# Exponentials of the experts' softmax taken as powers of e on GpSimd instead of Exp on ScalarE

## The chip, the cores and the metric

One Trainium2 chip, one of its cores. The time is the device time of one launch in microseconds (us), the median of several runs. Beside the runs there is one profiled execution, with a record of every instruction and transfer.

## What is computed

`x` has 4096 rows of 128 features, `adj` is a 4096 x 4096 matrix of zeros and ones. Two blocks follow one another, each a graph attention and a feed-forward part, each added to `x`:

```python
x = x + _L0_gnn_ref(_layernorm(x, axis=-1), adj, L0_gnn_Wq, L0_gnn_Wk)
x = x + _L0_ffn_ref(_layernorm(x, axis=-1)[None], ...)[0]      # 30 steps of tanh, silu, layernorm, matmul
x = x + _L1_gnn_ref(_layernorm(x, axis=-1), adj, L1_gnn_Wq, ...)
x = x + _L1_ffn_ref(_layernorm(x, axis=-1)[None], L1_ffn_W1, ...)[0]
```

The change is in the last part, a layer of 8 experts of which each row uses the likeliest:

```python
H = jax.nn.gelu(xf @ W1 + b1, approximate=False)               # 512 hidden features
probs = jax.nn.softmax((H @ Wg + bg) / TEMP, axis=-1)          # 8 experts
assign = jnp.argmax(probs, axis=-1)
out = jnp.zeros_like(xf)
for e in range(Wd.shape[0]):
    y = H @ Wd[e] + bd[e]
    sel = (assign == e)[:, None]
    out = out + jnp.where(sel, probs[:, e:e + 1] * y, 0.0)
```

## The kernel before, in words

Every engine has a program of its own, written out by hand, and runs it in order; semaphores join them. The 4096 rows are 8 chunks of 512 rows (4 tiles of 128). The program has a preparation, the attention of block one (tiles named `a_`), the 30 steps (`r_`), the attention of block two (`b_`), and then the experts (class `Experts`; tiles `x_`, and many tiles of the attention under new names: `b_p_s` holds the hidden layer, `b_prob` gelu's result, `b_p_r` logits, ranks and the products, `b_gathered` the logits of a chunk, experts along the partitions). The experts go through the rows twice.

**The first pass** decides for each row which expert it goes to. Chunk by chunk TensorE turns the normalised rows (`turn_rows`, L1524), multiplies them by W1 in three float16 products for each of 4 parts (`layer`, L1535 to L1537), multiplies gelu's result by Wg in float32 (`logits`, L1547), turns the logits (`turn_logits`, L1558) and counts ranks (`ranks`). ScalarE rounds the turned rows to float16 (`front`, L1636), takes four gelus (`gelu`, L1645), and, two chunks late, the exponentials of the shifted logits, 4 tiles x 8 experts = 32 columns (`exps(c)`, L1661). Gelu and exp are in different tables of ScalarE, so an ACT_TABLE_LOAD stands before each change. VectorE, in `vector`, does per turn `c` of its loop: `copy_logits(c-1)`, `rows_low(c+2)`, `places(c-2)`, `weigh(c-2)`, `choose(c-1)`, `rows(c+3)`. `choose` (L1728 to L1744) takes the maximum, writes `shifted` (L1735) and the chosen expert; `places` gives each row its place in the sorted order; `weigh` (L1765 to L1770) waits for the exponentials, sums them over the 8 experts, inverts the sum and writes it, as the gate, into the packed row.

GpSimd copies x into the packed rows (`copy_x`, L1900), inverts the deviations of the last chunk once VectorE has measured them (`invert_rows`, L153 to L158, the last of the three a power of 4 columns), and sends each chunk's rows to their places in memory: `send(c)` waits for `weighed` of the chunk, then issues four indirect DMAs (L1907). Its loop before:

```python
        invert_rows(k, self.x_stats, pool, CHUNKS - 1)
        for c in range(CHUNKS):
            if c + 2 < CHUNKS:
                copy_x(c + 2)
            send(c)
```

The chunks are in two sets, 0 to 2 and 3 to 7. When a set is sent and its table of tiles is made (`table`, on VectorE), the queue of SP loads the sorted rows of that set, group by group (`sync`, L1495 and L1496).

**The second pass** takes 13 groups of up to 4 tiles of sorted rows: turned, multiplied by W1 and through gelu again, split in a high and a low part (`highs` on ScalarE, L1654; `lows` on VectorE, L1821), multiplied by the weights of the one expert of each tile (`products` on TensorE, L1586 to L1592), weighted by the gate and added to x (`send_back`, L1831), and scattered to the output by GpSimd (`store`, L1914). At the seam of the passes ScalarE takes `exps(5)` before the first two gelus of group 0, `exps(6)` after them and `exps(7)` after the group's last high part; VectorE does `weigh(7)` and `table(1)` between the low parts of group 0 and those of group 1. One more exponential, the elu of the attention's last chunk (`elu(CHUNKS - 1)`, L804), is taken by ScalarE in the turn c == 1 of the first pass.

Of the kernel before, what the change touches and what calls it, by code (L numbers as in the profile page):

```python
# [19 lines left out]

# [1 line left out]

# [7 lines left out]
ALU = mybir.AluOpType  # L32
ACT = mybir.ActivationFunctionType
# [3 lines left out]
P = 128  # L37
# [4 lines left out]
CHUNKS = N // CHUNK  # L42
TPC = CHUNK // P
# [5 lines left out]
E = 8  # L49
# [98 lines left out]
def invert_rows(k, s, pool, g):  # L148

    nc = k.nc  # L150
    var, padded = s["variance"][:, 0], s["variance"][:, 1]
    pool.wait_ge(s["measured"], TPC // 2 * (g + 1))
    nc.gpsimd.tensor_tensor(var.rearrange("p (a b) -> p a b", b=2), k.x_stats[:, ds(TPC // 2 * g, TPC // 2), 2:6:3],  # L153
                            k.inv_d[:].rearrange("p (a b) -> p a b", b=2), ALU.mult).then_inc(s["inverting"], 1)
    pool.wait_ge(s["inverting"], 3 * g + 1)
    nc.gpsimd.tensor_tensor(padded, var, k.eps[:], ALU.add).then_inc(s["inverting"], 1)
    pool.wait_ge(s["inverting"], 3 * g + 2)
    nc.gpsimd.tensor_tensor(k.rstd[:, ds(TPC * g, TPC)], padded, k.minus_half[:], ALU.pow).then_inc(s["inverting"], 1)  # L158
    pool.wait_ge(s["inverting"], 3 * g + 3)
# [164 lines left out]
def normalise_a(k, adj, adj_in):  # L324
# [6 lines left out]
    nc, io = k.nc, k.io  # L331
    with ExitStack() as ctx:
# [10 lines left out]
        s = {n: k.sem("a_" + n, ctx) for n in names}  # L343
# [26 lines left out]
        def _(dve):  # L370
# [4 lines left out]
            nc.vector.memset(k.ones_bf[:], 1.0)  # L375
            nc.vector.memset(k.ones[:], 1.0)
            nc.vector.memset(k.shift[:], SHIFT)

            nc.vector.memset(k.row_hi[:, :, D - 1:D], 1.0)
            nc.vector.memset(k.row_lo[:, :, D - 1:D], 0.0)  # L380
# [1047 lines left out]
class Experts:  # L1428
# [199 lines left out]
    def scalar(self, act, elu):  # L1628
        k, s, nc = self.k, self.s, self.k.nc

        def front(n):
            act.wait_ge(s["ft_ready"], n + 1)
            if n > 1:
                act.wait_ge(s["h_ready"], HC * (n - 1))
            wide = slice(0, P * (TPC if n < CHUNKS else SPANS[n - CHUNKS]))
            nc.scalar.copy(self.f_hi[n % 2][:, wide], self.p_ft[n % 2][:, wide]).then_inc(s["ft_hi"], 1)  # L1636

        def gelu(n, h):
            act.wait_ge(s["h_ready"], HC * n + h + 1)
            if 1 < n < CHUNKS + 2:  # L1640
                act.wait_ge(s["lt_ready"], n - 1)
            elif n > 1:
                act.wait_ge(s["lo_ready"], HC * (n - 2 - CHUNKS) + h + 1)
            wide = slice(0, P * (TPC if n < CHUNKS else SPANS[n - CHUNKS]))
            nc.scalar.activation(self.hid[n % 2][h][:, wide], self.p_h[h][:, wide], ACT.Gelu, bias=k.b1[:, h:h + 1],  # L1645
                                 scale=k.e_unit[:, 3:4]).then_inc(s["gelu_ready"], 1)

        def highs(q, h):
            n = CHUNKS + q
            act.wait_ge(s["gelu_ready"], HC * n + h + 1)  # L1650
            if q > 1 and h == 0:
                act.wait_ge(s["y_ready"], q - 1)
            wide = slice(0, P * SPANS[q])
            nc.scalar.activation(self.hid_hi[q % 2][h][:, wide], self.hid[n % 2][h][:, wide], ACT.Copy,  # L1654
                                 scale=k.e_scale[:, 0:1]).then_inc(s["hi_ready"], 1)

        def exps(c):
            act.wait_ge(s["shifts"], c + 1)
            if c > 0:
                act.wait_ge(s["weighing"], 2 * c - 1)  # L1660
            nc.scalar.activation(self.expo[:], self.shifted[c % 2][:], ACT.Exp).then_inc(s["exps"], 1)  # L1661

        front(0)
        for h in range(HC):
            gelu(0, h)
            if h == 1:
                front(1)
        for c in range(CHUNKS - 1):
            if c + 2 < CHUNKS:
                front(c + 2)  # L1670
            if c > 1:
                exps(c - 2)
            for h in range(HC):
                gelu(c + 1, h)
            if c == 1:
                elu(CHUNKS - 1)
        front(CHUNKS)
        front(CHUNKS + 1)
        exps(CHUNKS - 3)
        gelu(CHUNKS, 0)  # L1680
        gelu(CHUNKS, 1)
        exps(CHUNKS - 2)
        for q in range(GROUPS):
            n = CHUNKS + q
            if q > 0:
                gelu(n, 0)
                gelu(n, 1)
            highs(q, 0)
            gelu(n, 2)
            highs(q, 1)  # L1690
            gelu(n, 3)
            highs(q, 2)
            if 0 < q < GROUPS - 1:
                front(n + 1)
            highs(q, 3)
            if q == 0:
                exps(CHUNKS - 1)

    def vector(self, dve, leave, finish):
        k, s, nc = self.k, self.s, self.k.nc  # L1700
# [195 lines left out]
    def gpsimd(self, pool, masks):  # L1896
        k, s, nc = self.k, self.s, self.k.nc

        def copy_x(c):
            nc.gpsimd.tensor_copy(self.pack[c][:, :, D:2 * D], k.x[:, TPC * c:TPC * c + TPC, :]).then_inc(s["x_copied"], 1)  # L1900

        def send(c):
            pool.wait_ge(s["x_copied"], c + 1)
            pool.wait_ge(s["f_ready"], c + 1)
            pool.wait_ge(s["weighed"], c + 1)
            for t in range(TPC):
                nc.gpsimd.indirect_dma_start(k.sorted, bass.IndirectOffsetOnAxis(self.to_place[c][:, t:t + 1], 0),  # L1907
                                             self.pack[c][:, t, :], None).then_inc(self.sent[SET_OF[c]], 16)

        def store(q):  # L1910
            par = q % 2
            for t in range(SPANS[q]):
                pool.wait_ge(s["done"], STARTS[q] + t + 1)
                nc.gpsimd.indirect_dma_start(k.io["out"], bass.IndirectOffsetOnAxis(self.to_row[par][:, t:t + 1], 0),  # L1914
                                             self.done[par][:, t, :], None, bounds_check=N - 1, oob_is_err=False)\
                    .then_inc(self.stored[par], 16)

        pool.wait_ge(k.blanked, 16 * (BLANKS + E))
        pool.wait_ge(self.attended["masked"], masks // 2)
        copy_x(0)  # L1920
        copy_x(1)
        invert_rows(k, self.x_stats, pool, CHUNKS - 1)
        for c in range(CHUNKS):
            if c + 2 < CHUNKS:
                copy_x(c + 2)
            send(c)
        for q in range(GROUPS):
            store(q)
        for q in (GROUPS - 2, GROUPS - 1):
            pool.wait_ge(self.stored[q % 2], self.stored_by(q))  # L1930


def build(nc, io):

    with ExitStack() as ctx:
        k = Core(nc, ctx, io)
# [19 lines left out]
        k.ones_bf = k.sb("ones_bf", [P, P], BF16)  # L1956
        k.minus_half, k.eps, k.eps_sum, k.inv_d = (k.sb(n, [P, TPC]) for n in ("minus_half", "eps", "eps_sum", "inv_d"))
        k.shift = k.sb("shift", [P, 1])
        k.w_ffn = k.sb("w_ffn", [P, D])
        k.bias_ffn = k.sb("bias_ffn", [P, TPC, D], BF16)  # L1960
        k.bias_mid = k.sb("bias_mid", [1, D], BF16)
# [76 lines left out]
```

## Time and profile before

| | us |
|---|---|
| median of 3 runs | 1434.35 (1434.26, 1434.35, 1439.12) |
| the profiled execution, its own time | 1429.9 |
| its span, first to last instruction | 1428.1 |
| mean granted TensorE clock | 0.974 |

In the span the experts lie at the end: the first gelu's table is loaded at 1250.9 us and the last indirect DMA of the output is issued at 1419.1 us. Times in the trace's rows are us from the start of the span. A busy TensorE is not TensorE at its peak, and a row's idle time belongs to the engine, not to the program: only what ends last in a stretch counts there. "issue" is time in which an engine waited for nothing that the profile shows.

### The profile page before, as it was taken

How to read it: one execution, taken by the hardware profiler on the slowest of the kernel's cores; microseconds unless marked ns; L12 is line 12 of the kernel's file. 1: busy time of each engine (PE TensorE's matmuls, PEld its weight loads, DVE VectorE, ACT ScalarE, POOL GpSimd, SP SyncE). 2: the span in 40 equal slices, each digit the busy share in tenths (PEclk: the TensorE clock that was granted, in tenths of full speed). 3: DMA queues.
4: the chain of work that ended last, by engine and by line, in shares of the span. 5: the costliest groups of instructions: out<-in, count | busy, mean ns of one | idle time of the engine just before them, and what ended most of it. 6: DMA issues, size and time to landing. Idle time of an engine off the chain costs nothing. (4 is left out here: it accounts for less than half of the span.)

```text
span 1428.1 us, 27595 instructions
## 1 busy us (share of the span) xinstructions
PE 1294.5 (91%) x7723; PEld 793.7 (56%) x7723; DVE 1280.7 (90%) x2230; ACT 1131.4 (79%) x1774; POOL 841.3 (59%) x1071
## 2 busy tenths in 40 slices
PE   5699999999985999999999996999999999899895
PEld 4444444444434888888888884344444444333664
DVE  7699999999997999999999998789999999966753
ACT  5677777676765999999999996787888778767773
POOL 4264665666658999999999996123323333216554
PEclk9899999999997999999999998999999999999997
DMA  7054555554528993000000000455555555204330
GB/s 263 1 203 180 187 196 177 176 202 180 182 83 294 334 330 120 0 0 0 0 0 0 0 0 1 148 199 184 193 190 197 188 200 182 84 2 144 95 91 24
DMA packets 65798, 186.76 MB, mean 131 GB/s; under 512 B 4515, under 2 KB 47539, under 8 KB 49234
## 3 DMA queue, kind: packets, MB, share of 16 engines
q1 hardware_dynamic: 62738, 179.74, 37.0%
q0 software_dynamic: 3008, 6.37, 1.3%
q8 instruction: 27, 0.44, 0.1%
q14 instruction: 25, 0.20, 0.0%
HBM read 145.51 MB, written 41.49 MB: 131 GB/s over the span
## 5 line engine op out<-in xcount | busy, mean ns | idle before, releaser
L1060 PEld LDWEIGHTS r_p_y<-w_ffn,r_z_t 128*128 128x128 f32 x1920 | 255.7, 194 | 6.7
L1060 PE MATMUL r_p_y<-w_ffn,r_z_t 128*128 128x128 f32 x1920 | 255.6, 277 | 0.0
L1271 POOL TENSOR_TENSOR r_stat<-r_stat,minus_half 128x4 f32<-128x4 f32 x240 | 244.2, 1018 | 18.8
L831 POOL TENSOR_TENSOR b_lo<-b_prob,b_hi 128x1024 f16<-128x1024 f32 x32 | 80.0, 2499 | 251.7 <-ACT b_hi L800 251.7
L897 DVE SCALAR_TENSOR_TENSOR b_prob<-adj_rows,b_prob 128x1024 f32<-128x1024 int32 x128 | 188.1, 1473 | 25.5 <-ACT b_prob L793 25.2
L897 DVE SCALAR_TENSOR_TENSOR a_prob<-adj_rows,a_prob 128x1024 f32<-128x1024 int32 x128 | 192.3, 1506 | 13.5 <-ACT a_prob L793 13.5
L793 ACT ACTIVATE b_prob<-b_p_s,shift,g_unit 128x1024 f32<-128x1024 f32 x128 | 154.0, 1203 | 53.0 <-PE b_p_s L722 52.8
L793 ACT ACTIVATE a_prob<-a_p_s 128x1024 f32<-128x1024 f32 x128 | 130.9, 1023 | 70.4 <-PE a_p_s L722 70.4
L1196 DVE BATCH_NORM_STATS2 r_parts<-r_z 128x6 f32<-128x256 f32 x480 | 182.1, 421 | 0.0
L831 POOL TENSOR_TENSOR a_lo<-a_prob,a_hi 128x1024 f16<-128x1024 f32 x32 | 87.4, 2730 | 144.1 <-ACT a_hi L800 144.1
L1189 DVE SCALAR_TENSOR_TENSOR r_h<-r_tanh,r_p_y 128x512 f32<-128x512 f32 x232 | 158.8, 684 | 3.6 <-ACT r_tanh L1128 0.9
L800 ACT CAST a_hi<-a_prob 128x1024 f16<-128x1024 f32 x128 | 133.3, 1041 | 34.8 <-DVE a_prob L897 32.4
L1048 PE MATMUL r_p_t<-early,a_start 128*128 128x128 f32 x960 | 146.7, 276 | 9.8 <-DVE a_start L1202 9.8
L1132 ACT ACTIVATE r_z<-r_h 128x512 f32<-128x512 f32 x240 | 150.4, 626 | 4.6 <-DVE r_h L1189 4.6
L1145 ACT COPY r_z_t<-r_p_t 128x512 f32<-128x512 f32 x240 | 138.0, 575 | 8.6 <-PE r_p_t L1048 8.6
L800 ACT CAST b_hi<-b_prob 128x1024 f16<-128x1024 f32 x128 | 132.6, 1036 | 14.7 <-DVE b_prob L897 14.1
L1128 ACT ACTIVATE r_tanh<-r_p_y 128x512 f32<-128x512 f32 x232 | 138.8, 598 | 1.0 <-PE r_p_y L1060 0.9
L905 DVE TENSOR_TENSOR a_lo<-a_prob,a_hi 128x1024 f16<-128x1024 f32 x96 | 131.3, 1368 | 0.0
L1048 PEld LDWEIGHTS r_p_t<-early,a_start 128*128 128x128 f32 x960 | 114.9, 143 | 11.0 <-DVE a_start L1202 10.5
L905 DVE TENSOR_TENSOR b_lo<-b_prob,b_hi 128x1024 f16<-128x1024 f32 x96 | 116.5, 1214 | 0.8
L1202 DVE TENSOR_TENSOR a_start<-r_z,r_stat 128x256 f32<-128x256 f32 x240 | 114.2, 476 | 0.0
L733 PE MATMUL a_p_o<-a_hi,row_hi 128*128 128x512 f16 x256 | 97.3, 380 | 18.4 <-DVE a_lo L905 16.3
(289 smaller groups left out, 3023.0 us busy)
## 6 DMA issues: line engine op xcount, KB each, us to landing
adj_rows<-in_adj_t SPq DMA_DIRECT2D x128, 1024.0 KB, 4.8
sorted_rows<-blank SPq DMA_DIRECT2D x7, 4160.0 KB
x_got<-sorted_rows SPq DMA_DIRECT2D x46, 130.0 KB
sorted_rows<-blank SPq DMA_DIRECT2D x1, 4290.0 KB
x_rows<-in_x SPq DMA_DIRECT2D x4, 512.0 KB, 8.7
wd_raw<-in_wd SPq DMA_DIRECT2D x1, 2048.0 KB, 10.0
late<-in_late SPq DMA_DIRECT2D x1, 756.0 KB
out_x<-b_rows,x_to_row POOLq DMA_INDIRECT x46
```

Of the source, the lines that this page charges most:

```text
L793: nc.scalar.activation(prob[st][:], p_s[st % 2][:], ACT.Exp, bias=0.0 if is_a else k.shift[:, 0:1], scale=1.0 / UNIT ** 2 if is_a else k.g ...
L800: nc.scalar.copy(hi[st][:], prob[st][:]).then_inc(s["hi_ready"], 1)
L831: nc.gpsimd.tensor_tensor(lo[POOL_STEP][:], prob[POOL_STEP][:], hi[POOL_STEP][:], ALU.subtract).then_inc(s["lo_pool_ready"], 1)
L897: nc.vector.scalar_tensor_tensor(prob[st][:], adj[transfer % ADJ][:, st % 2, :], 0.0, prob[st][:], ALU.is_gt, ALU.mult).then_inc(s["masked ...
L905: nc.vector.tensor_tensor(lo[st][:], prob[st][:], hi[st][:], ALU.subtract).then_inc(s["lo_ready"], 1)
L1048: last = nc.tensor.transpose(p_t[g % TB][:, P * t:P * t + P], z_unit[g][:, D * t:D * t + D], k.ident[:])
L1060: last = nc.tensor.matmul(out[:, D * t:D * t + D], z_t[g % R][:, P * t:P * t + P], k.w_ffn[:], start=False, stop=(t == TPC - 1), skip_grou ...
L1128: nc.scalar.activation(tanh[g % R][:], p_y[g % YB][:], ACT.Tanh).then_inc(s["tanh_ready"], 1)
L1132: nc.scalar.activation(z[g][:], h[g % R][:], ACT.Silu).then_inc(s["z_ready"], 1)
L1189: nc.vector.scalar_tensor_tensor(h[g % R][:], tanh[g % R][:], 0.01, before, ALU.mult, ALU.add)\
L1196: last = nc.vector.bn_stats(parts[g][:, i, :], tiles(z[g])[:, 2 * i:2 * i + 2, :].rearrange("p t d -> p d t"))
L1271: nc.gpsimd.tensor_tensor(stat[g][:, 1, :], stat[g][:, 0, :], k.minus_half[:], ALU.pow)\
```

## The change

The eight `exps` go from ScalarE's program to GpSimd's. `exp(v)` is computed as `e ** v`: a tile `euler` of 32 columns filled with e (one more memset at the start of VectorE's program) is raised to the shifted logits by a GpSimd tensor_tensor with the operation pow. In GpSimd's loop `exps(c)` stands after `copy_x(c + 2)` and before `send(c)`; `invert_rows` is moved behind `exps(0)`. The semaphores are the same. The elu's exponential stays on ScalarE.

```diff
--- before.py
+++ after.py
@@ -20,6 +20,7 @@
 
 
 
+import math
 from contextlib import ExitStack
 
 import concourse.bass as bass
@@ -375,6 +376,7 @@
             nc.vector.memset(k.ones_bf[:], 1.0)
             nc.vector.memset(k.ones[:], 1.0)
             nc.vector.memset(k.shift[:], SHIFT)
+            nc.vector.memset(k.euler[:], math.e)
 
             nc.vector.memset(k.row_hi[:, :, D - 1:D], 1.0)
             nc.vector.memset(k.row_lo[:, :, D - 1:D], 0.0)
@@ -1654,12 +1656,6 @@
             nc.scalar.activation(self.hid_hi[q % 2][h][:, wide], self.hid[n % 2][h][:, wide], ACT.Copy,
                                  scale=k.e_scale[:, 0:1]).then_inc(s["hi_ready"], 1)
 
-        def exps(c):
-            act.wait_ge(s["shifts"], c + 1)
-            if c > 0:
-                act.wait_ge(s["weighing"], 2 * c - 1)
-            nc.scalar.activation(self.expo[:], self.shifted[c % 2][:], ACT.Exp).then_inc(s["exps"], 1)
-
         front(0)
         for h in range(HC):
             gelu(0, h)
@@ -1668,18 +1664,14 @@
         for c in range(CHUNKS - 1):
             if c + 2 < CHUNKS:
                 front(c + 2)
-            if c > 1:
-                exps(c - 2)
             for h in range(HC):
                 gelu(c + 1, h)
             if c == 1:
                 elu(CHUNKS - 1)
         front(CHUNKS)
         front(CHUNKS + 1)
-        exps(CHUNKS - 3)
         gelu(CHUNKS, 0)
         gelu(CHUNKS, 1)
-        exps(CHUNKS - 2)
         for q in range(GROUPS):
             n = CHUNKS + q
             if q > 0:
@@ -1693,8 +1685,6 @@
             if 0 < q < GROUPS - 1:
                 front(n + 1)
             highs(q, 3)
-            if q == 0:
-                exps(CHUNKS - 1)
 
     def vector(self, dve, leave, finish):
         k, s, nc = self.k, self.s, self.k.nc
@@ -1915,14 +1905,24 @@
                                              self.done[par][:, t, :], None, bounds_check=N - 1, oob_is_err=False)\
                     .then_inc(self.stored[par], 16)
 
+        def exps(c):
+
+            pool.wait_ge(s["shifts"], c + 1)
+            if c > 0:
+                pool.wait_ge(s["weighing"], 2 * c - 1)
+            nc.gpsimd.tensor_tensor(self.expo[:].rearrange("p t e -> p (t e)"), k.euler[:],
+                                    self.shifted[c % 2][:].rearrange("p t e -> p (t e)"), ALU.pow).then_inc(s["exps"], 1)
+
         pool.wait_ge(k.blanked, 16 * (BLANKS + E))
         pool.wait_ge(self.attended["masked"], masks // 2)
         copy_x(0)
         copy_x(1)
-        invert_rows(k, self.x_stats, pool, CHUNKS - 1)
         for c in range(CHUNKS):
             if c + 2 < CHUNKS:
                 copy_x(c + 2)
+            exps(c)
+            if c == 0:
+                invert_rows(k, self.x_stats, pool, CHUNKS - 1)
             send(c)
         for q in range(GROUPS):
             store(q)
@@ -1956,6 +1956,7 @@
         k.ones_bf = k.sb("ones_bf", [P, P], BF16)
         k.minus_half, k.eps, k.eps_sum, k.inv_d = (k.sb(n, [P, TPC]) for n in ("minus_half", "eps", "eps_sum", "inv_d"))
         k.shift = k.sb("shift", [P, 1])
+        k.euler = k.sb("euler", [P, TPC * E])
         k.w_ffn = k.sb("w_ffn", [P, D])
         k.bias_ffn = k.sb("bias_ffn", [P, TPC, D], BF16)
         k.bias_mid = k.sb("bias_mid", [1, D], BF16)
```

GpSimd's program where the experts begin (`b_variance` and `rstd` are tiles of `invert_rows`, `x_expo` the exponentials, `sorted_rows` the memory that the rows are sent to). Before:

```order
L1900 COPY adj_rows<-x_rows 128x4x128 [waits b_masked,blanked]
L1900 COPY adj_rows<-x_rows 128x4x128
L153 TENSOR_TENSOR b_variance<-x_stats,inv_d 128x4 [waits b_measured]
L156 TENSOR_TENSOR b_variance<-b_variance,eps 128x4 [waits b_inverting]
L158 TENSOR_TENSOR rstd<-b_variance,minus_half 128x4 [waits b_inverting]
L1900 COPY adj_rows<-x_rows 128x4x128 [waits b_inverting]
L1907 DMA sorted_rows<-adj_rows,x_to_place 32896x260 [waits x_weighed,x_f_ready,x_x_copied]
L1907 DMA sorted_rows<-adj_rows,x_to_place 32896x260 x3
L1900 COPY adj_rows<-x_rows 128x4x128
L1907 DMA sorted_rows<-adj_rows,x_to_place 32896x260 [waits x_weighed,x_f_ready,x_x_copied]
```

After:

```order
L1890 COPY adj_rows<-x_rows 128x4x128 [waits b_masked,blanked]
L1890 COPY adj_rows<-x_rows 128x4x128 x2
L1913 TENSOR_TENSOR x_expo<-euler,x_shifted 128x32 [waits x_shifts]
L154 TENSOR_TENSOR b_variance<-x_stats,inv_d 128x4 [waits b_measured]
L157 TENSOR_TENSOR b_variance<-b_variance,eps 128x4 [waits b_inverting]
L159 TENSOR_TENSOR rstd<-b_variance,minus_half 128x4 [waits b_inverting]
L1897 DMA sorted_rows<-adj_rows,x_to_place 32896x260 [waits x_f_ready,x_weighed,x_x_copied,b_inverting]
L1897 DMA sorted_rows<-adj_rows,x_to_place 32896x260 x3
L1890 COPY adj_rows<-x_rows 128x4x128
L1913 TENSOR_TENSOR x_expo<-euler,x_shifted 128x32 [waits x_weighing,x_shifts]
L1897 DMA sorted_rows<-adj_rows,x_to_place 32896x260 [waits x_weighed,x_f_ready,x_x_copied]
L1897 DMA sorted_rows<-adj_rows,x_to_place 32896x260 x3
```

A power that waits for VectorE's shifts stands ahead of each send, the first also ahead of the inversion of the deviations; a send waits for `x_weighed`, and VectorE's `weigh` behind that waits for the power.

ScalarE's program from `front(8)` and `front(9)`, at the seam of the passes, on. Before:

```order
L1636 CAST mov_hi<-b_p_o 128x512 [waits x_h_ready,x_ft_ready] x2
L1661 ACT_TABLE_LOAD [waits x_weighing]
L1661 ACTIVATE x_expo<-x_shifted 128x32 [waits x_shifts]
L1645 ACT_TABLE_LOAD [waits x_lt_ready]
L1645 ACTIVATE b_prob<-b_p_s,late,e_unit 128x512 [waits x_h_ready]
L1645 ACTIVATE b_prob<-b_p_s,late,e_unit 128x512 [waits x_lt_ready,x_h_ready]
L1661 ACT_TABLE_LOAD [waits x_weighing]
L1661 ACTIVATE x_expo<-x_shifted 128x32 [waits x_shifts]
L1654 ACTIVATE sta_hi<-b_prob,e_scale 128x512 [waits x_gelu_ready]
L1645 ACT_TABLE_LOAD [waits x_lt_ready]
L1645 ACTIVATE b_prob<-b_p_s,late,e_unit 128x512 [waits x_h_ready]
L1654 ACTIVATE sta_hi<-b_prob,e_scale 128x512 [waits x_gelu_ready]
```

After:

```order
L1638 CAST mov_hi<-b_p_o 128x512 [waits x_h_ready,x_ft_ready] x2
L1647 ACTIVATE b_prob<-b_p_s,late,e_unit 128x512 [waits x_lt_ready,x_h_ready] x2
L1656 ACTIVATE sta_hi<-b_prob,e_scale 128x512 [waits x_gelu_ready]
L1647 ACTIVATE b_prob<-b_p_s,late,e_unit 128x512 [waits x_lt_ready,x_h_ready]
L1656 ACTIVATE sta_hi<-b_prob,e_scale 128x512 [waits x_gelu_ready]
L1647 ACTIVATE b_prob<-b_p_s,late,e_unit 128x512 [waits x_lt_ready,x_h_ready]
L1656 ACTIVATE sta_hi<-b_prob,e_scale 128x512 [waits x_gelu_ready] x2
```

The exponentials are gone, and with seven of the eight a load of exp's table before and of gelu's table behind. Of 17 table loads in the experts' part 3 are left: gelu at the start, exp for the elu, and gelu behind it.

## Rows read from the trace of the kernel before

**Rows 1.** The page of the kernel before: busy time by engine

```profile
PE 1294.5 (91%) x7723; PEld 793.7 (56%) x7723; DVE 1280.7 (90%) x2230; ACT 1131.4 (79%) x1774; POOL 841.3 (59%) x1071
```

**Rows 2.** Three stretches: us, busy PE PEld DVE ACT POOL, granted clock, DMA share, GB/s

```profile
1250.00:1312.00 62.00, 56.98 (x309) 22.38 (x306) 41.64 (x172) 43.22 (x58) 25.77 (x32) 1.00 0.19 59
1312.00:1332.00 20.00, 16.58 (x124) 8.95 (x125) 15.45 (x64) 18.84 (x26) 11.94 (x13) 0.91 0.41 128
1332.00:1380.00 48.00, 45.33 (x410) 30.74 (x408) 30.60 (x67) 35.12 (x59) 24.50 (x25) 1.00 0.33 91
```

**Rows 3.** TensorE in order of time, first pass: start us, us, engine line op

```profile
1279.86 0.64 PE L1524 MATMUL b_p_o<-early,adj_rows 128*128 128x128 f32 x4
...
1287.25 0.64 PE L1524 MATMUL b_p_o<-early,adj_rows 128*128 128x128 f32 x4
```

**Rows 4.** ScalarE in order of time, the same turn (in brackets: idle before, releaser)

```profile
1282.42 0.23 ACT L1661 ACTIVATE x_expo<-x_shifted 128x32 f32<-128x32 f32 x1
1282.67 1.28 ACT L1645 ACT_TABLE_LOAD   x1
1283.97 2.78 ACT L1645 ACTIVATE b_prob<-b_p_s,late,e_unit 128x512 f32<-128x512 f32 x4
1287.92 0.58 ACT L1636 CAST mov_hi<-b_p_o 128x512 f16<-128x512 f32 x1 [1.17 <-PE b_p_o L1524]
```

**Rows 5.** Groups of instructions, ScalarE, 1200 to 1429 us: count | busy us, mean ns | idle

```profile
L1645 ACT ACT_TABLE_LOAD x9 | 11.5, 1283 | 0.3 <-PE b_p_r L1547 0.2
...
L1661 ACT ACT_TABLE_LOAD x7 | 9.0, 1283 | 0.1
```

**Rows 6.** The chain that ended last, in order of time, between the two passes

```profile
1317.88 1.28 ACT L1661
```

**Rows 7.** GpSimd in order of time, first pass (DMA_INDIRECT: one of the four sends of a chunk)

```profile
1280.71 0.20 POOL L153 TENSOR_TENSOR b_variance<-x_stats,inv_d 128x4 f32<-128x4 f32 x1 [28.81 <-DVE x_stats L144]
...
1281.27 1.01 POOL L158 TENSOR_TENSOR rstd<-b_variance,minus_half 128x4 f32<-128x4 f32 x1
1282.33 0.61 POOL L1900 COPY adj_rows<-x_rows 128x512 f32<-128x512 f32 x1
1283.28 1.31 POOL L1907 DMA_INDIRECT sorted_rows<-adj_rows,x_to_place  x1 [0.34 <-POOL adj_rows L1900]
...
1301.61 0.98 POOL L1907 DMA_INDIRECT sorted_rows<-adj_rows,x_to_place  x1 [1.48 <-DVE adj_rows L1770]
...
1306.42 0.62 POOL L1900 COPY adj_rows<-x_rows 128x512 f32<-128x512 f32 x1
```

**Rows 8.** VectorE in order of time: shifts of chunk 0, then sums and gates

```profile
1269.12 0.19 DVE L1735 TENSOR_TENSOR x_shifted<-x_logit,x_red 128x32 f32<-128x32 f32 x1
...
1275.17 0.18 DVE L1765 TENSOR_REDUCE x_red<-x_expo 128x4 f32<-128x32 f32 x1
...
1290.08 0.18 DVE L1765 TENSOR_REDUCE x_red<-x_expo 128x4 f32<-128x32 f32 x1
...
1300.08 0.17 DVE L1765 TENSOR_REDUCE x_red<-x_expo 128x4 f32<-128x32 f32 x1
...
1300.58 0.23 DVE L1770 TENSOR_SCALAR adj_rows<-x_red,e_back 128x4 f32<-128x4 f32 x1
```

**Rows 9.** Groups of instructions, GpSimd, whole span: a power and a sum of 4 columns

```profile
L1271 POOL TENSOR_TENSOR r_stat<-r_stat,minus_half 128x4 f32<-128x4 f32 x240 | 244.2, 1018 | 18.8
...
L1268 POOL TENSOR_TENSOR r_stat<-r_parts,eps_sum 128x4 f32<-128x4 f32 x240 | 49.7, 207 | 4.3 <-DVE r_parts L1196 4.3
```

**Rows 10.** VectorE in order of time, from the sums of the last chunk on

```profile
1326.33 0.18 DVE L1765 TENSOR_REDUCE x_red<-x_expo 128x4 f32<-128x32 f32 x1
...
1332.11 0.75 DVE L1821 SCALAR_TENSOR_TENSOR sta_lo<-b_prob,e_scale,sta_hi 128x512 f16<-128x512 f32 x1 [0.17 <-ACT sta_hi L1654]
```

**Rows 11.** VectorE in order of time, beside a power and beside a copy of GpSimd

```profile
1282.05 0.18 DVE L1756 TENSOR_TENSOR x_place<-x_place,x_one_hot 128x32 f32<-128x32 f32 x1
...
1282.49 0.48 DVE L1760 CAST x_to_place<-x_red 128x4 int32<-128x4 f32 x1
```

## The prediction, made before the changed kernel was run

> **What bounds the kernel now.** I begin with the page: every engine but GpSimd is busy for 79% of the span or more [rows 1], which says little, since only the experts' part changes. So I cut that part into stretches [rows 2]. In the first pass (1250 to 1312 us) TensorE is busy 57 of 62 us; the order in time shows why: one turn begins with L1524 at 1279.86 and the next at 1287.25, 7.39 us later [rows 3]. In the same turn ScalarE loads a table, takes a 0.23 us exponential, loads the other table, takes its four gelus and still sits idle 1.17 us until TensorE lets it go on [rows 4]. **In the first pass the table loads are hidden.** At the seam of the passes (1312 to 1332 us) ScalarE is busy 18.84 of 20 us [rows 2], and the chain that ended last runs through a load itself [rows 6]: there three exponentials and six loads (the pairs for chunks 5, 6 and 7) bound. From 1332 us on TensorE is busy 45.3 of 48 us again [rows 2].
>
> GpSimd is busy only 26 of the first 62 us [rows 2], but that hides its shape. It waits 28.8 us for the last chunk's statistics, takes the power for them (1.01 us, to 1282.28), and starts the first send at 1283.28; from then on it sends. A chunk's four DMAs take 4.8 us (1301.61 to the copy at 1306.42), the copy behind them 0.62 us, and where a send waited for VectorE's gate it starts 0.80 us after it (gate at 1300.58 + 0.23 = 1300.81, DMA at 1301.61) [rows 7, 8].
>
> **What is removed.** ScalarE loses 8 exponentials of 0.23 us [rows 4] and 14 of its 17 table loads (7 of 7 of L1661, 7 of 9 of L1645), each 1.28 us [rows 5]: 1.8 + 18.0 = 19.8 us of its time. Most of it lies in the first pass, behind TensorE. On the path is only what lies at the seam, 6 x 1.28 + 3 x 0.23 = 8.4 us, and that only if nothing else is late there.
>
> The gelus after a load start 0.02 us after it ends (1282.67 + 1.28 = 1283.95, gelu at 1283.97) [rows 4]. The Trainium skill, ScalarE: Activation LUTs, What ACT_TABLE_LOAD costs, has every switch at 1283 ns and a drain of about 1380 ns besides. By that the 14 loads would be 37 us instead of 18 us; the trace agrees with the load and shows no drain, so I stay with the rows.
>
> **What is added.** Eight powers of 32 columns on GpSimd. No row has one. What there is: a power of 4 columns takes 1.018 us, a sum of 4 columns of the same shape 0.207 us, in 240 instances each [rows 9]. From below, 32 columns cannot be cheaper than 4: 1.02 us. From above, eight times the 4-column power: 8.14 us. In between I charge what the power has over the sum, 0.811 us, to its columns, and the 0.207 us to the instruction: 0.21 + 8 x 0.811 = 6.7 us. I take 6.7: the two rows differ in nothing but the operation, the extra is the arithmetic itself, and arithmetic is done for each column. VectorE's memset of 32 columns stands before the first statistics, where VectorE waits for x to arrive: nothing.
>
> **What is moved, and who queues behind it.** The power of chunk c stands behind the four DMAs of chunk c-1 and ahead of its own. VectorE stops in `weigh(c)` until it is done, and behind `weigh(c)` are `choose(c+1)`, the normalised rows, and the copies of the logits, for all of which TensorE waits. So a loop closes that was not there before: power, 0.05 to VectorE, gate 0.73 (1300.08 to 1300.81) [rows 8], 0.80 to the first DMA, 4.8 of DMAs, 0.62 of copy [rows 7], 0.08 to the next power. Without the power this is 7.1 us; with 6.7 it is **13.8 us per chunk** against TensorE's 7.39 [rows 3].
>
> Worked through, in the trace's own times. Chunk 0: the shifts are ready at 1269.12 + 0.19 = 1269.31, the power runs from 1269.4 to 1276.1; VectorE wanted it at 1275.17 [rows 8], so it is 0.9 us late, and with it the statistics. The power of the deviations ends at 1282.28 + 0.9 = 1283.2 and, the copy now being ahead of it, the first send starts 0.2 us later: 1283.4. The power of chunk 1 ends 4.8 + 0.62 + 0.08 + 6.7 = 12.2 us later, 1295.6. Six more turns of 13.8 us, two of them without a copy (chunks 6 and 7 have none, -1.24 us), put the end of the power of chunk 7 at 1295.6 + 82.8 - 1.2 = 1377.2. Before, VectorE began that chunk's sums at 1326.33 [rows 10]. That is 50.9 us later. From there VectorE makes the table and the low parts, which before followed with 0.17 us of idle time for ScalarE [rows 10]; that is the 0.2 us given back, since ScalarE is long done. So **the whole gain of 8.4 us at the seam is swallowed**, and the second pass, TensorE's, follows as it was: +50.7 us. The chunks' send of set 0, the loads of SP behind it and the stores all lie in the same shift. Against the profiled execution (1429.9 us) this makes 1480.6; the median of the runs is 4.45 us above that execution, so 1434.35 + 50.7 = **1485 us**.
>
> The same sum with the other prices: at 1.02 us the turn is 8.1 us, the first send starts at 1282.5, the last power ends at 1282.5 + 6.5 + 48.7 - 1.2 = 1336.5, +10.1; besides, VectorE's line from one `weigh` to the next is 10.0 us long where it makes the first table (1290.08 to 1300.08) [rows 8], 1.9 more than the turn: +12.0, 1446 us. At 8.14 us: turn 15.2, first send 1284.8, +62, 1496 us. Each microsecond of the power is worth about seven.
>
> **The rivals.**
> (a) The power is mostly launch, or works on several columns at once: 1.0 to 1.5 us, +12 to +16 us, 1446 to 1450. For it: nothing shows that the 0.811 us belongs to columns. Against: the sum, launched alike, has 0.207.
> (b) In between, 1.5 to 6 us: 1450 to 1480, the middle (3.8 us, turn 10.9) being +29, 1464.
> (c) The port. While GpSimd's copy ran (1282.33 to 1282.94) a conversion of VectorE took 0.48 us and ended with it; but a VectorE product of two tiles started at 1282.05 and took its 0.18 us while the power of 1281.27 to 1282.28 was still running [rows 7, 11]. So a short power does not keep VectorE out, and a long one, reading 32 columns, may. Then the rest of `choose(0)`, which follows the shifts at 1269.31 at once, stands still until 1276.1, and the statistics behind it come some 6 us late instead of 0.9: 5 us more, 1490. The Trainium skill, SBUF — State Buffer, Who interferes with whom, has that port as an exclusive lock, held for the whole instruction against VectorE's operations with two inputs in SBUF. That is this rival; the product at 1282.05 speaks against it for 4 columns.
> (d) TensorE's clock. It was granted in full in the first pass, and 0.91 at the seam, where it idled more [rows 2]. With 6 us idle in each turn it may fall to the lower of its levels (1.2 of 2.4 GHz); a turn of TensorE would then be 14.8 us instead of 7.39, 1 us over the loop: +6, 1491.
> (e) On the other side: the power hides in GpSimd's idle time, and ScalarE's 8.4 us at the seam come free: 1426 us, no slower, even faster. It decides where the loop falls under TensorE's turn: 7.1 + p < 7.39, p under 0.3 us. The 4-column power alone is 1.01 us, so only if a power of 32 columns were cheaper than one of 4.
> (f) That the change does not do what it says: the listing of the instructions shows 3 loads left and eight powers, so no.
>
> **How the numbers follow.** Forecast, power at 6 to 8.1 us: 52%. (b) 22%, (a) 12%, (c) 6%, (d) 6%, (e) 2%. The range reaches from the price of the 4-column power to eight times it, 1446 to 1496 us, and takes in (c) and (d); the forecast alone would be 1478 to 1496. A change of 0.5%, 7.2 us, is about what a measurement of this kernel can tell from none: all but (e) are slower by more, and (e) is split: faster 1%, same 1%, slower 98%.
>
> **What would show it.** Right: eight powers of about 6.7 us on GpSimd; the longest new wait is VectorE's for `x_expo`, 6 to 9 us each turn from chunk 1 on; successive powers 13.8 us apart; ScalarE with three table loads and long waits; sends of the last chunk some 50 us later, the second pass as long as before. Wrong: powers of 1 to 2 us and turns near 8 us (a); VectorE's operations beside the first power stretched to its end (c); a granted clock near half in the first pass with TensorE never idle (d); no wait for `x_expo` (e).

## The result, and the profile after

| | before | after |
|---|---|---|
| median of 4 runs | 1435.92 (1434.26 to 1439.12) | 1473.38 (1470.10 to 1477.61) |
| profiled execution, its own time | 1429.9 | 1472.72 |
| its span | 1428.1 | 1470.9 |
| mean granted TensorE clock | 0.974 | 0.964 |

The changed kernel is slower: ratio 1.026, 95% interval 1.0226 to 1.0294, +37.5 us between the medians and +42.8 us between the two profiled executions. The page of the kernel after, busy time by engine (before: [rows 1]):

```profile
PE 1288.4 (88%) x7662; PEld 795.8 (54%) x7723; DVE 1280.2 (87%) x2231; ACT 1112.3 (76%) x1752; POOL 882.6 (60%) x1079
```

ScalarE lost 19.1 us of work and GpSimd gained 41.3, eight powers of 5.46 us among it (43.7). Neither number is the cost: of the others only TensorE's weight loads have more to do, 2.1 us, and the span is 42.8 us longer. Stretches of the kernel after, with the columns of [rows 2]:

```profile
1250.00:1312.00 62.00, 45.88 (x233) 18.89 (x234) 31.94 (x131) 25.86 (x36) 32.60 (x24) 0.91 0.06 22
...
1332.00:1372.00 40.00, 21.26 (x146) 11.38 (x146) 16.09 (x69) 12.31 (x19) 30.55 (x19) 0.75 0.14 48
1372.00:1420.00 48.00, 42.42 (x373) 28.20 (x373) 29.84 (x68) 32.54 (x53) 26.31 (x26) 0.93 0.33 91
```

TensorE, busy 57 of the first 62 us before, is now busy 46, and 21 of the 40 us from 1332 on. In these 40 us VectorE is idle for 24 and ScalarE for 28, GpSimd for 9.5. From 1372 on TensorE is back at work. The waits of the kernel after, 1245 to 1475 us (who waited for whom: us in total, times, longest):

```profile
DVE x_red L1755 <- POOL x_expo L1913: 49.2, 7, 11.1
...
PE b_p_r L1570 <- DVE x_one_hot L1734: 28.5, 6, 8.9
```

VectorE waits for the power in seven chunks of eight, and TensorE for the choice that stands behind it in VectorE's program. So the other engines wait for GpSimd. GpSimd in order of time, kernel after (before: [rows 7]; left out are three of the four sends of each chunk and the turns alike):

```profile
1270.29 5.43 POOL L1913 TENSOR_TENSOR x_expo<-euler,x_shifted 128x32 f32<-128x32 f32 x1 [16.93 <-DVE x_shifted L1725]
...
1282.17 1.01 POOL L159 TENSOR_TENSOR rstd<-b_variance,minus_half 128x4 f32<-128x4 f32 x1
1283.50 1.30 POOL L1897 DMA_INDIRECT sorted_rows<-adj_rows,x_to_place  x1 [0.32 <-POOL rstd L159]
...
1288.60 0.62 POOL L1890 COPY adj_rows<-x_rows 128x512 f32<-128x512 f32 x1
1289.18 5.47 POOL L1913 TENSOR_TENSOR x_expo<-euler,x_shifted 128x32 f32<-128x32 f32 x1
1296.23 1.05 POOL L1897 DMA_INDIRECT sorted_rows<-adj_rows,x_to_place  x1 [1.59 <-DVE adj_rows L1760]
...
1301.12 0.62 POOL L1890 COPY adj_rows<-x_rows 128x512 f32<-128x512 f32 x1
1301.70 5.46 POOL L1913 TENSOR_TENSOR x_expo<-euler,x_shifted 128x32 f32<-128x32 f32 x1
...
1363.45 5.46 POOL L1913 TENSOR_TENSOR x_expo<-euler,x_shifted 128x32 f32<-128x32 f32 x1
```

This is the loop: copy, power, 1.59 us of waiting until the gate is back and the DMA starts, four DMAs. From the power at 1289.18 to the next at 1301.70 are **12.52 us**; from the second power to the eighth are 74.27. VectorE in order of time, kernel after (before: [rows 8, 10]), shows the other half of it:

```profile
1276.08 0.18 DVE L1755 TENSOR_REDUCE x_red<-x_expo 128x4 f32<-128x32 f32 x1
...
1294.68 0.19 DVE L1755 TENSOR_REDUCE x_red<-x_expo 128x4 f32<-128x32 f32 x1 [11.12 <-POOL x_expo L1913]
...
1296.53 0.19 DVE L1734 TENSOR_TENSOR x_one_hot<-x_chosen,x_red 128x32 bf16<-128x32 f32 x1
...
1368.95 0.19 DVE L1755 TENSOR_REDUCE x_red<-x_expo 128x4 f32<-128x32 f32 x1 [6.79 <-POOL x_expo L1913]
```

Chunk 0's sums were not late (the power ended at 1275.72, they began at 1276.08). Those of the last chunk begin at 1368.95, before at 1326.33 [rows 10]: 42.6 us later, the whole difference of the two executions (42.8). So behind it no more than 0.2 us was lost, and of the time ahead 0.9 us was there before the first power (the shifts of chunk 0 at 1270.02, before at 1269.12 [rows 8]). Of the rest 10.9 us were lost at chunk 1 alone: its sums came 18.6 us after those of chunk 0 (1276.08 to 1294.68), before 7.7, since its power stands behind chunk 0's sends and these behind the last chunk's statistics.

### The profile page after: what moved, and what is told of

It reads as the page before. It is cut to its first block and busy times, and to the rows that moved or that the text cites. A ratio compares the mean times of both kernels' runs of the same rounds, so it can differ in the third digit from the quotient of the medians.

```text
span 1470.9 us, 27522 instructions
## 1 busy us (share of the span) xinstructions
PE 1288.4 (88%) x7662; PEld 795.8 (54%) x7723; DVE 1280.2 (87%) x2231; ACT 1112.3 (76%) x1752; POOL 882.6 (60%) x1079
```

## The experiments

Times are medians; each batch ran beside the kernel before on the same chip: 1435.11 us for the first (scalar_copy, tanh, ladder), 1435.42 for the second (pool_add, pow_twice, pow_aside, pow_ahead), 1434.05 for the third (pow_half, pow_quarter). "+" is against that batch's own before. The diffs show the lines that carry an edit; most of the semaphore calls that go with them are left out, and "..." marks other lines left out.

### Is a table load at the seam worth anything? scalar_copy and tanh

```diff
-            nc.scalar.activation(self.expo[:], self.shifted[c % 2][:], ACT.Exp)
+            nc.scalar.activation(self.expo[:], self.shifted[c % 2][:], ACT.Copy)
```

> The kernel before with the eight exponentials of the experts taken as plain copies on ScalarE (a copy is in every table, so 14 table loads go; gates are wrong, places and all else are as before). It prices the table loads by themselves. The prediction's term: 8.4 us of them bound at the seam of the passes, so about 1427.5 us against 1435.9 (-0.6%). Rival: VectorE was as late there as ScalarE (in the trace of before it works without a gap from 1319.4 us on to the low parts of group 1), so the loads are worth 0 to 1.5 us: 1434.4 to 1435.9.

Measured: 1434.94 us (12 runs), ratio 1.0001 (0.9987 to 1.0015). The 14 loads are gone and the time is the same. Before, the chain ran through ScalarE's loads at the seam ([rows 6]). In scalar_copy, ScalarE in order of time at the same place:

```profile
1320.45 0.23 ACT L1661 ACTIVATE x_expo<-x_shifted 128x32 f32<-128x32 f32 x1 [2.02 <-DVE x_shifted L1735]
...
1326.07 0.23 ACT L1661 ACTIVATE x_expo<-x_shifted 128x32 f32<-128x32 f32 x1 [1.61 <-DVE x_shifted L1735]
```

and its VectorE and TensorE:

```profile
1323.30 0.68 DVE L1723 COPY b_gathered<-b_p_r 8x512 f32<-8x512 f32 x1 [2.12 <-PE b_p_r L1547]
...
1326.73 2.73 DVE L1821 SCALAR_TENSOR_TENSOR sta_lo<-b_prob,e_scale,sta_hi 128x512 f16<-128x512 f32 x4
```

```profile
1319.67 3.60 PE L1547 MATMUL b_p_r<-b_prob,late 128*8 128x512 f32 x8
...
1330.04 0.22 PE L1586 MATMUL b_p_r<-bd_parts,ones_bf 3*128 x1 [2.17 <-DVE sta_lo L1821]
```

ScalarE now waits for VectorE's shifts where it had loads to make. The chain goes from TensorE's logits of the last chunk (3.6 us) through VectorE's places, gates and low parts to the products. VectorE's part of it is as long as before: from the copy of those logits (L1723) to the low parts (L1821) are 1326.73 - 1323.30 = 3.43 us here, and 1322.86 - 1319.44 = 3.42 in the kernel before, where VectorE worked without a gap too. The whole piece, from the start of the logits to the first product (L1586), takes 10.37 us. The same two rows in the kernel before and in ladder, a run further down that keeps all the loads:

```profile
1315.80 3.60 PE L1547 MATMUL b_p_r<-b_prob,late 128*8 128x512 f32 x8
...
1327.10 0.22 PE L1586 MATMUL b_p_r<-bd_parts,ones_bf 3*128 x1 [2.01 <-issue]
```

```profile
1320.80 3.60 PE L1549 MATMUL b_p_r<-b_prob,late 128*8 128x512 f32 x8
...
1331.19 0.22 PE L1588 MATMUL b_p_r<-bd_parts,ones_bf 3*128 x1 [2.19 <-DVE sta_lo L1823]
```

With all its loads ladder needs 10.39 us, as long as scalar_copy without them; both had a granted clock of 0.83 from 1310 to 1320 us, and their logits began late. The profiled execution of before had 1.00 there and began early; it needs 11.30, so there the loads may have cost the 0.9 us between. So VectorE's chain is about as long as ScalarE's, and the view shows but the one that ended last. The rival of this expectation held.

```diff
-            nc.scalar.activation(self.expo[:], self.shifted[c % 2][:], ACT.Exp)
+            nc.scalar.activation(self.expo[:], self.shifted[c % 2][:], ACT.Tanh, scale=0.5)
...
+            nc.vector.tensor_scalar(self.below[:], expo[:], -1.0, 1.0, ALU.mult, ALU.add)
+            nc.vector.reciprocal(self.below[:], self.below[:])
+            nc.vector.tensor_reduce(red[:, 2, :], self.below[:], AX.X, ALU.add)
+            nc.vector.tensor_scalar(red[:, 2, :], red[:, 2, :], 2.0, -float(E), ALU.mult, ALU.add)
```

> The kernel before with exp(v) = 2/(1 - tanh(v/2)) - 1: tanh is in gelu's table, so 14 loads go, and VectorE gets three more small operations for each chunk (about 0.65 us). If the loads are worth 8.4 us: -6 to -8 us, 1428 to 1430. If VectorE's line is the one that binds at the seam: +0.5 to +2.5 us, 1436.5 to 1438.5.

Measured: 1436.46 us (11 runs), ratio 1.0009 (0.9997 to 1.0021). Here the aim of the change is reached in another way, exp(v) = 2 / (1 - tanh(v / 2)) - 1, with tanh in gelu's table and three more short operations of VectorE per chunk. The 14 loads go, and nothing is gained: that is next to what was expected if VectorE's line is the one that binds (1436.5 to 1438.5), and far from what loads worth 8.4 us would have given (1428 to 1430).

### What does a power cost? ladder

```diff
+        for n in (1, 4, 8, 16, 32, 64):
+            nc.gpsimd.tensor_tensor(k.spare[:, at:at + n], k.euler[:, 0:n], k.halves[:, 0:n], ALU.pow)
+            at += n
```

(and one with the exponents 1 to 8 in `ranks`, and a product of 32 columns; all before GpSimd's first work for the experts is due, and read by nobody).

> The kernel before with eight more GpSimd operations, results unused, where GpSimd waits before the first send: powers e ** -0.5 of 1, 4, 8, 16, 32 and 64 columns, e ** (1 to 8) of 32 columns, and a product of 32 columns. If the cost is a launch and so much a column, through the 4-column power (1.02) and the 32-column one (5.46): 0.54, 1.02, 1.65, 2.9, 5.46, 10.5 us. If it works on several columns at once (blocks of 8 or 16): steps, with 1 and 4 columns alike, or 8 and 16. The prediction's rule (0.21 + 0.203 a column): 0.41, 1.02, 1.83, 3.5, 6.7, 13.2. Exponents 1 to 8 cost as -0.5 does, unless the time goes by the values. The product: 0.25 us. Time as before, if the ladder of some 27 us ends before the statistics are there; up to 2 us more if not.

The kernel took 1435.3 us. Groups of instructions of ladder by shape, GpSimd, 1250 to 1284 us (columns as in [rows 9]):

```profile
L1926 POOL TENSOR_TENSOR spare<-euler,halves 128x64 f32<-128x64 f32 x1 | 10.5, 10545 | 0.0
L1926 POOL TENSOR_TENSOR spare<-euler,halves 128x32 f32<-128x32 f32 x1 | 5.5, 5460 | 0.0
L1928 POOL TENSOR_TENSOR spare<-euler,late 128x32 f32<-128x32 f32 x1 | 5.4, 5426 | 0.0
L1926 POOL TENSOR_TENSOR spare<-euler,halves 128x16 f32<-128x16 f32 x1 | 2.9, 2902 | 0.0
...
L1926 POOL TENSOR_TENSOR spare<-euler,halves 128x8 f32<-128x8 f32 x1 | 1.6, 1641 | 0.0
...
L1926 POOL TENSOR_TENSOR spare<-euler,halves 128x4 f32<-128x4 f32 x1 | 1.0, 1029 | 0.0
L1929 POOL TENSOR_TENSOR spare<-euler,halves 128x32 f32<-128x32 f32 x1 | 0.8, 782 | 0.0
L1926 POOL TENSOR_TENSOR spare<-euler,halves 128x1 f32<-128x1 f32 x1 | 0.6, 552 | 0.0
```

The price is a line: (10.545 - 1.029) / 60 = 0.159 us per column and 0.39 us besides. It does not depend on the exponents tried (-0.5, and the ranks 1 to 8: 5.46 and 5.43). A product of 32 columns took 0.78 us here, and a subtraction of 32 took 0.25 us in pool_add, so a product standing behind a power is no clean price.

The same run answers the rival of the port. From 1253.9 to 1281.2 us GpSimd did nothing but powers, and VectorE beside it, in order of time:

```profile
1271.27 0.18 DVE L1738 TENSOR_TENSOR x_chosen<-x_logit,x_red 128x32 f32<-128x32 f32 x1
1271.49 0.19 DVE L1740 TENSOR_TENSOR x_chosen<-x_chosen,late 128x32 f32<-128x32 f32 x1
```

These are operations with two inputs from SBUF in the middle of the 64-column power, and they have the length of those with no power beside them (0.18 to 0.19 us). A conversion at 1277.14, beside the next power, took its usual 0.17 us.

### What does the place cost, and each microsecond in it? pool_add, pow_quarter, pow_half, pow_twice

The four keep the changed kernel's order and waits and change only how long the instruction is.

```diff
-                                    self.shifted[c % 2][:].rearrange("p t e -> p (t e)"), ALU.pow).then_inc(s["exps"], 1)
+                                    self.shifted[c % 2][:].rearrange("p t e -> p (t e)"), ALU.subtract).then_inc(s["exps"], 1)
```

> The changed kernel with a difference (e - shifted) in place of the power, all else in its place: the gates are wrong, the rest is the same. It prices the place without the power. Loop theory: the turn is 7.1 + 0.25 = 7.35 us, but chunk 1's small operation still stands behind the four sends of chunk 0, which wait for the last chunk's statistics, so VectorE is some 5 us late from there, and up to 2 us more where it makes the first table: +5 to +7.5 us, 1441 to 1443.5. If only the operation's price counts (eight times 5.2 us less on the path) and the place is free: 1473 - 42 = 1431, or lower by the table loads.

pow_quarter and pow_half (with 16 for 8) against the change:

```diff
+        nc.vector.memset(expo[:].rearrange("p t e -> p (t e)")[:, 8:], 1.0)
...
-            nc.gpsimd.tensor_tensor(self.expo[:].rearrange("p t e -> p (t e)"), k.euler[:],
+            nc.gpsimd.tensor_tensor(self.expo[:].rearrange("p t e -> p (t e)")[:, 0:8], k.euler[:, 0:8],
...
```

> The same with the power of the first 8 columns only (the other 24 are 1.0, so the gates of three quarters of the tokens are wrong); 8 columns took 1.64 us in the width test. Theory: a turn of 8.7 us, still over TensorE's 7.39, so 7 x 3.82 = 26.7 us under the changed kernel, 1446.7; the straight line gives 1449.8. I expect 1445 to 1451. Rival (knee): no more than the subtraction of 0.25 us costs, 1441 to 1443.

> The changed kernel with the power taken of the first 16 of the 32 columns; the other 16 columns of x_expo are set to 1.0 once, so the gates of half of the tokens are wrong. The width test gave 2.90 us for 16 columns. Theory (GpSimd's turn is 7.1 us plus the power, and seven turns lie on the path): the turn falls from 12.52 to 10.0 us and the time by 7 x 2.56 = 17.9 us, to 1455.5; a straight line between the two points measured so far (1441.2 at 0.25 us, 1473.4 at 5.46 us: 6.2 us per us) gives 1457.6. I expect 1454 to 1459. Rival (a knee: what is not GpSimd's power in the turn has room of its own, and a short power hides in it): 1446 or less.

pow_twice, ahead of the power of each chunk:

```diff
+            nc.gpsimd.tensor_tensor(self.spare[:], k.euler[:],
+                                    self.shifted[c % 2][:].rearrange("p t e -> p (t e)"), ALU.pow)
```

> The changed kernel with each power taken twice (first into a spare tile). Loop theory: turn 12.5 + 5.5 = 18 us, seven turns' worth (+38) and chunk 0's power now 5 us late for VectorE: +43 over the changed kernel, 1516 to 1520. If part of a power is hidden behind other work in each turn: less than 38 more, under 1505.

| kernel | length, us | median, us | runs | ratio (interval) | against before | chunk 0's shifts to chunk 7's sums, us |
|---|---|---|---|---|---|---|
| before | | | | | | 57.2 |
| pool_add | 0.25 | 1441.17 | 10 | 1.0047 (1.0027 to 1.0067) | +5.8 | 64.8 |
| pow_quarter | 1.67 | 1450.82 | 4 | 1.0111 (1.0089 to 1.0134) | +16.8 | 72.9 |
| pow_half | 2.94 | 1456.87 | 4 | 1.0156 (1.0137 to 1.0175) | +22.8 | 81.3 |
| the change | 5.46 | 1473.38 | 4 | 1.026 (1.0226 to 1.0294) | +37.5 | 98.9 |
| pow_twice | 10.88 | 1517.58 | 2 | 1.0571 (1.0529 to 1.0613) | +82.2 | 141.6 |

The last column is read from the profiled executions. The medians of the four experiments lie in what was expected. From the first to the last they are 76.4 us apart for 10.63, 7.2 us per us, but the slope is not the same all along: 6.1 from pool_add to the change, 8.2 from there to pow_twice. In pow_twice the power of chunk 0 is late as well, and VectorE waits 4.97 us for it:

```profile
1281.54 0.19 DVE L1756 TENSOR_REDUCE x_red<-x_expo 128x4 f32<-128x32 f32 x1 [4.97 <-POOL x_expo L1916]
```

Without these 4.97 the last column gives (141.6 - 98.9 - 5.0) / 5.42 = 7.0 us per us, and from pow_half to the change 7.0 too: seven turns. Below that it is less (5.7 from pool_add to pow_quarter), since VectorE does not wait for so short a power in every turn: 5 times in pool_add, 6 in pow_quarter, 7 in the change. No stretch is flat, so there is no knee, no length that would be free. GpSimd of pow_half and pow_twice in order of time, two powers each:

```profile
1300.89 2.93 POOL L1914 TENSOR_TENSOR x_expo<-euler,x_shifted 128x16 f32<-128x16 f32 x1
1310.88 2.98 POOL L1914 TENSOR_TENSOR x_expo<-euler,x_shifted 128x16 f32<-128x16 f32 x1
```

```profile
1317.75 5.42 POOL L1916 TENSOR_TENSOR x_expo<-euler,x_shifted 128x32 f32<-128x32 f32 x1
1335.71 5.42 POOL L1916 TENSOR_TENSOR x_expo<-euler,x_shifted 128x32 f32<-128x32 f32 x1
```

The turns are 9.99 us (7.1 + 2.93 = 10.03) and 17.96 (7.1 + 10.88 = 17.98). And pool_add shows that the place alone costs: at 0.25 us the turn is 7.34, no longer than TensorE's, and still the time is 5.8 us more. The first send of chunks 1 to 3, GpSimd in order of time:

```profile
1293.02 1.00 POOL L1897 DMA_INDIRECT sorted_rows<-adj_rows,x_to_place  x1 [1.58 <-DVE adj_rows L1760]
...
1300.36 1.00 POOL L1897 DMA_INDIRECT sorted_rows<-adj_rows,x_to_place  x1 [1.58 <-DVE adj_rows L1760]
...
1309.91 1.01 POOL L1897 DMA_INDIRECT sorted_rows<-adj_rows,x_to_place  x1 [3.70 <-DVE adj_rows L1760]
```

The first of these turns is 7.34 us; the second is 9.55, since VectorE makes the first set's table there. That is no loss: VectorE's line was 10.0 us long there before, too (1290.08 to 1300.08 [rows 8]). The loss lies at chunk 1, in VectorE's program:

```profile
1291.47 0.18 DVE L1755 TENSOR_REDUCE x_red<-x_expo 128x4 f32<-128x32 f32 x1 [5.91 <-POOL x_expo L1913]
```

VectorE stands 5.91 us for an operation of 0.25 us that is queued behind chunk 0's four sends, which themselves wait for the last chunk's statistics. Chunk 1's sums come 13.4 us after those of chunk 0 (1278.08), before 7.7; at the last chunk the delay is 7.6 us (64.8 instead of 57.2), so it is not made up.

### The queue or the loop? pow_aside and pow_ahead

In pow_aside (made from the kernel before) the sums use ScalarE's exponentials as before; GpSimd takes the power of the same shifts in the same place, for nobody. In pow_ahead (made from the changed kernel) the power is used, and the one of chunk c+1 stands ahead of the sends of chunk c.

```diff
+            nc.gpsimd.tensor_tensor(self.spare[:, c], k.euler[:],
+                                    self.shifted[c][:].rearrange("p t e -> p (t e)"), ALU.pow)\
+                .then_inc(s["spared"], 1)
...
+            spare_power(c)
+            if c == 0:
+                invert_rows(k, self.x_stats, pool, CHUNKS - 1)
             send(c)
```

```diff
-            exps(c)
+            if c == 0:
+                exps(0)
+            if c + 1 < CHUNKS:
+                exps(c + 1)
...
             send(c)
```

> The loop opened: ScalarE takes the exponentials as before, table loads and all, and GpSimd takes the same power at the same place into a tile that nobody reads (it waits for the shifts alone; the shifts have a tile for each chunk, so nobody waits for it). GpSimd's work a chunk is 4.8 + 0.62 + 5.46 + 0.3 = 11.2 us without a wait. If the loss is the closed loop (VectorE and TensorE standing for the power): VectorE is not held in the first pass, the last exponentials come about 10 us later than before through the first set's later rows, and only the late sends of the second set and stores behind them cost more: +15 to +20 in all, 1451 to 1456, half of the change's loss. If the loss is GpSimd's work alone: as the changed kernel, 1470 or more.

> The changed kernel with the power of chunk c+1 ahead of the sends of chunk c, so that the four sends stand beside VectorE's work instead of ahead of the power. Turn: GpSimd's work alone, 5.46 + 4.8 + 0.62 + 0.3 = 11.2 us instead of 12.5, and chunk 1's power no longer waits for the statistics (5 us). Loop theory: +20 to +26 over before, 1456 to 1462, 11 to 17 less than the changed kernel. If the order on GpSimd is of no matter: 1473.

Measured: pow_aside 1461.79 us (4 runs), ratio 1.0185 (1.0153 to 1.0218), +26.4, more than my theory for it and less than its rival; pow_ahead 1457.66 (4 runs), 1.0145 (1.0112 to 1.0178), +22.2, as expected, and 15.3 less than the change's 37.5. GpSimd of pow_aside and of pow_ahead in order of time, one turn each, of pow_ahead also the power of chunk 1:

```profile
1302.08 5.46 POOL L1922 TENSOR_TENSOR x_spare<-euler,x_shifted 128x32 f32<-128x32 f32 x1
...
1313.17 5.46 POOL L1922 TENSOR_TENSOR x_spare<-euler,x_shifted 128x32 f32<-128x32 f32 x1
```

```profile
1281.36 5.43 POOL L1913 TENSOR_TENSOR x_expo<-euler,x_shifted 128x32 f32<-128x32 f32 x1 [1.97 <-DVE x_shifted L1725]
...
1305.57 5.58 POOL L1913 TENSOR_TENSOR x_expo<-euler,x_shifted 128x32 f32<-128x32 f32 x1
1311.35 1.06 POOL L1897 DMA_INDIRECT sorted_rows<-adj_rows,x_to_place  x1 [0.20 <-issue]
...
1316.79 5.47 POOL L1913 TENSOR_TENSOR x_expo<-euler,x_shifted 128x32 f32<-128x32 f32 x1
```

Both turns are about 11.1 us (11.09 and 11.22): copy 0.62, power 5.46, 0.2 to the first send, 4.8 of sends, with no wait in them. **GpSimd is then full, and that alone is more than TensorE's 7.39.** I had reckoned pow_aside's delay too low; its waits, 1245 to 1475 us, say who pays:

```profile
PE b_p_o L1526 <- DMA x_got<-sorted_rows: 21.3, 3, 9.0
```

TensorE reaches the second pass and the sorted rows are not there. It does so for both sets: the sends of chunk 2, the last of the first set, end at 1312.6 us, before at 1299.5, and the last chunk's start at 1362.16, before at 1328.0 (2.7 us of either were there before the first power). From chunk 0's shifts to chunk 7's sums are 69.9 us, 12.7 more than before (10 were expected); the rest comes behind. So a power that nobody waits for costs 26 us through the sends behind it, by another route than the change's (there TensorE waited for VectorE, and VectorE for the power).

The 15.3 us by which pow_ahead is better than the change have two parts. The power of chunk 1 runs at 1281.36, ahead of chunk 0's sends, while GpSimd would wait for the statistics: from chunk 0's sums to chunk 2's are 20.1 us instead of 31.1, 11.0 less. The change's own turn is 1.4 us longer than the full queue, the way of the gate through VectorE and back (1.59 of waiting instead of 0.20); over the five turns from chunk 2's sums to chunk 7's this makes 6.1 us (55.7 instead of 61.8). Together these are 17.1 us in the profiled executions. pow_ahead comes out 4 us under pow_aside, but their intervals overlap.

## Why the prediction was right, and where it was off

The time lay in the range, and the direction was right; the forecast was 11.6 us too high, and the case that came was rival (b), a power in between, to which I gave 22%. The loop, the mechanism of the sum, is what the runs show. That the time fell into the range is worth little by itself: the range is 50 us wide.

- **"I take 6.7"** is the term that was off: measured 5.46 us. It gave the whole 0.811 us that the 4-column power has over the sum to the columns, 0.203 each. The line of ladder gives 0.159 per column and leaves 0.39 us that are paid once: a power has more fixed time than a sum (0.207). Two rows cannot part slope from offset, so 8 x the small power and the small power alone were honest ends, and the middle a choice. In seven turns the 1.24 us are 8.7.
- **"7.1 us plus the power"** held in four kernels: 12.52 (sum 12.56), 9.99, 17.96, 7.34. With 5.46 in the same working the second and the eighth power are 6 x 12.56 - 1.24 = 74.1 us apart; measured 74.27.
- **"Each microsecond of the power is worth about seven"**: 7.0 in the traces from pow_half up, less for shorter powers; by the medians 6.1 from 0.25 to 5.46 us.
- **"0.9 us late"** for chunk 0: nothing, the power being short enough.
- **"8.4 us on the path at the seam"** was wrong, though the sum did not use it, since the loop swallowed it. Left alone, the loads give back 0.0 us (scalar_copy, tanh). I had taken the load in the chain of waits for its price. Rival (e), 1426 us, was built on it and could not have come even with a free power.
- **The median.** I added the 4.45 us by which the kernel's runs lay above its profiled execution to the new time. The profiled execution of after lies only 0.7 us under its own median, so 3.8 us of the miss are that step: against the profiled execution I said 1480.6, it was 1472.7. With the 8.7 above these are 12.5 of a miss of 11.6; the 0.9 us of chunk 0 that did not come and the 0.9 us that the two executions were apart before the experts cancel. The 0.9 us too many are small rows: the second power ended 0.3 us later than the working with 5.46 has it (chunk 0's four DMAs took 5.1 us, 1283.50 to 1288.60, where I had 4.8), the turns made 0.15, and behind the last sums 0.2 us were lost where I had 0.2 given back.
- **Page on the table load.** The Trainium skill, ScalarE: Activation LUTs, What ACT_TABLE_LOAD costs, has a drain beside the load's 1283 ns; no run here shows one, and without the loads no time came back.
- **Rival (c), the port**: not so. In the change too, VectorE's operations beside the first power have their normal length but one (L1728, 0.24 instead of 0.19 us). By the Trainium skill, SBUF — State Buffer, Who interferes with whom, they would have stood still until the power ended; measured, they did not, for 32 nor for 64 columns.
- **Rival (d), the clock**: it did fall, to 0.91 in the first pass and 0.75 from 1332 to 1372 us, but the loop and not TensorE still set the turn. The kernel after, TensorE in order of time, after the wait for the choice of chunk 2:

```profile
1296.78 0.22 PE L1570 MATMUL b_p_r<-x_one_hot,before_row 128*128 128x8 bf16 x2 [8.93 <-DVE x_one_hot L1734]
```

and two stretches behind that wait, with the columns of [rows 2]:

```profile
1296.70:1300.60 3.90, 3.33 (x23) 2.06 (x24) 2.62 (x10) 0.94 (x2) 2.98 (x4) 0.51 0.24 86
1300.60:1306.00 5.40, 5.40 (x21) 1.55 (x18) 1.10 (x3) 2.53 (x4) 5.40 (x3) 1.00 0.12 39
```

After 8.9 us of waiting TensorE works at the lower of its levels (0.51, 1.2 GHz) for some 4 us and then at the full one. At half speed these cost it 2 us, in a turn of 12.52 us with 7.39 us of work.

## What to carry to other kernels

Price work moved to an "idle" engine by its turn, not by its busy share: GpSimd was busy 26 of 62 us, but 28.8 of the idle ones lay ahead of the first send, and per chunk it had 7.39 - 5.6 = 1.8 us left (copy and sends are 5.4, and 0.2 between), which a 5.5 us operation cannot fit. If the result goes back through an engine that others wait for, add the round trip. And before a switch is paid for, take it away by itself (any other function that is in the table already): here the saving was zero, and two runs say so. Look also at what the new place stands behind the first time round: here 5.9 us were lost at chunk 1 even with an operation of 0.25 us.

## What the runs showed of the hardware

- GpSimd's power of float32 on 128 partitions: 0.55, 1.03, 1.64, 2.90, 5.46 and 10.55 us for 1, 4, 8, 16, 32 and 64 columns; a subtraction of 32 columns 0.25 us. ScalarE's exponential of the same 32 columns takes 0.23 us, a pair of table loads included 2.8.
- GpSimd's power does not hold up VectorE, but its sends and copies do: VectorE's product L1746 in the kernel after, beside the fourth send of chunk 1, which ran from 1300.15 to 1301.11, and the conversion behind it beside the copy:

```profile
1300.48 0.66 DVE L1746 TENSOR_TENSOR x_place<-x_place,x_one_hot 128x32 f32<-128x32 f32 x1
...
1301.40 0.38 DVE L1750 CAST x_to_place<-x_red 128x4 int32<-128x4 f32 x1
```

The product, with both inputs in SBUF, usually takes 0.18 us and ended with the send, at 1301.14; the conversion usually takes 0.17 and ended with the copy. Two operations with one input in SBUF (L1742 and L1745, at 1300.19 and 1300.40), beside the same send, kept their 0.18 and 0.16 us. The stretched ones are few and cost less than 1 us a turn. What the send and the copy hold, and the power does not, no run here parts.
